# Attention on one core: unnormalised exponentials turned, heads as rows of tokens

## The reference

```python
q = einsum('bnd,hdk->bhnk', layernorm(x), proj_q) + bias_q      # k, v the same from the context
logits = einsum('bhqk,bhnk->bhqn', q, k) / 8
attn = softmax(logits, axis=-1)                                  # over 154 keys
heads = einsum('bhqn,bhnv->bhqv', attn, v)
x = x + heads_as_rows(heads) @ w_out.T
x = x + ffn(layernorm(x))       # 4-bit quantised inputs and weights in three products
```

## Time and profile before

| | us |
|---|---|
| median of 3 runs | 429.55 (426.49 to 430.19) |
| the profiled execution | 429.8 |
| its span | 427.9 |

### The profile page before, as it was taken

The page is one execution under the profiler, slowest core; times in us unless marked ns, Lnnn a source line. Parts: engine busy times, 40 slices in busy tenths (PEclk is TensorE's granted clock), DMA queues, the critical chain, the costliest instruction groups (busy, mean ns, idle before and its releaser), DMA issues.

```text
span 427.9 us, 9077 instructions
## 1 busy us (share of the span) xinstructions
PE 337.4 (79%) x3371; PEld 250.3 (58%) x3371; DVE 363.5 (85%) x652; ACT 259.6 (61%) x821; POOL 273.2 (64%) x275
## 2 busy tenths in 40 slices
PE   1865877876969969869687698198877999999985
PEld 1542355665747757757465466076655766677764
DVE  2989558899999997999999969448999999999692
ACT  4756578877787877877884678334351545543331
POOL 3453455897888878978886568613592767686710
PEclk9999589998998979999999669689998999999999
DMA  7970343455554464655543434600000000000001
GB/s 218 323 282 1 63 92 63 82 105 96 93 102 86 93 117 86 109 84 91 106 85 73 93 63 92 123 2 2 2 0 15 12 26 12 21 19 12 27 25 38
DMA packets 92413, 32.44 MB, mean 76 GB/s; under 512 B 84492, under 2 KB 90320, under 8 KB 92369
## 3 DMA queue, kind: packets, MB, share of 16 engines
q1 hardware_dynamic: 92369, 31.86, 34.7%
HBM read 8.78 MB, written 2.10 MB: 25 GB/s over the span
## 4 chain that ended last, share of the span: by engine, by line
DVE 58%; PE 18%; POOL 14%; issue 5%; ACT 3%; DMA 1%; SPq 0%; DVEq 0%; POOLq 0%
DVE negmax L1036 6%; POOL arena L1304 5%; POOL arena L1298 5%; DVE arena L1049 5%; DVE arena L1055 4%; DVE arena L1112 4%; DVE arena L1114 4%; DVE arena L998 3%; PE ps L456 3%; PE ps L458 3%; PE ps L591 3%; PE ps L457 3%; DVE arena L1027 3%; DVE arena L1238 3%; DVE blk_h L1069 2%
## 5 line engine op out<-in xcount | busy, mean ns | idle before, releaser
L805 ACT ACTIVATE arena<-ps,negmax 128x154 f32<-128x154 f32 x256 | 96.5, 395 | 46.8 <-DVE negmax L1036 46.5
L1297 POOL TENSOR_TENSOR arena<-arena,rinv 128x104 f32<-128x104 f32 x64 | 30.1, 470 | 64.5 <-DVE rinv L1042 64.5
L1298 POOL TENSOR_TENSOR arena<-arena,rinv 128x512 f32<-128x512 f32 x64 | 70.5, 1102 | 0.0
L1036 DVE TENSOR_REDUCE negmax<-ps 128x4 f32<-128x616 f32 x64 | 50.2, 785 | 20.5 <-PE ps L591 20.3
L1304 POOL TENSOR_TENSOR arena<-arena 128x640 f16<-128x640 f32 x40 | 63.7, 1592 | 0.8 <-ACT arena L816 0.8
L591 PE MATMUL ps<-kT_h,arena 64*128 64x154 f16 x512 | 39.8, 241 | 28.6 <-DVE arena L1027 18.7
L805 ACT ACTIVATION_READ_ACCUMULATOR arena<-ps,negmax 128x1 f32 x256 | 53.8, 210 | 0.0
L591 PEld LDWEIGHTS ps<-kT_h,arena 64*128 64x128 f16 x512 | 24.0, 98 | 44.9 <-DVE arena L1027 27.0
L456 PE MATMUL ps<-arena,xnT_h 128*128 128x352 f16 x128 | 40.1, 313 | 3.2 <-DVE xnT_l L1122 3.2
L456 PE MATMUL ps<-xnT_h,wq_h 128*128 128x256 f16 x128 | 36.2, 283 | 7.9 <-DVE wot_l L984 2.5
L456 PE MATMUL ps<-arena 128*128 128x256 f16 (+2 forms) x120 | 36.1, 301 | 7.8 <-DVE arena L937 5.9
(11 more groups left out here) (155 smaller groups left out, 1030.5 us busy)
## 6 DMA issues: line engine op xcount, KB each, us to landing
out_dram<-arena SPq DMA_DIRECT2D x16, 128.0 KB, 1.7
xs<-in_x_dram SPq DMA_DIRECT2D x2, 512.0 KB, 7.2
arena<-in_L_xattn_w_out_dram SPq DMA_DIRECT2D x1, 1024.0 KB, 11.8
pT<-arena SPq DMA_TRANSPOSE x64, 3.4
xs<-in_x_dram SPq DMA_DIRECT2D x2, 384.0 KB, 6.6
wffn<-in_L_ffn_w_down_dram SPq DMA_DIRECT2D x1, 704.0 KB, 9.5
wffn<-in_L_ffn_w_gate_dram SPq DMA_DIRECT2D x1, 640.0 KB, 7.8
wffn<-in_L_ffn_w_up_dram SPq DMA_DIRECT2D x1, 640.0 KB, 8.4
```

The source lines that it names most:

```text
L805: last = act.activation(prob[:, j, k * L:(k + 1) * L], ps[:, 2 * (j % 2) + k % 2, (k // 2) * L:(k // 2 + 1) * L], ACT.Exp, bias=negmax[:, ...
L1036: dve.tensor_reduce(negmax[:, s, 4 * j:4 * j + 4].rearrange("p (k u) -> p u k", k=2), v, AX.X, ALU.max, negate=True).then_inc(max_done, 1)
L1298: pool.tensor_tensor(main_of(normal, j), v[:, :, 0:P], r.to_broadcast([P, 4, P]), ALU.mult).then_inc(normed, 1)
```

## The change

Probabilities stay unnormalised: `exps` writes exp(score - max) for each head into 160 columns (154 and 6 zeros), without sums. ACT casts each slot's 128x640 (`high_p`, now all on ACT, from `prob`), POOL subtracts (`low_p`, all on POOL), SP turns it as before, 5 chunks of 128 columns in which heads lie across borders. `norm` and the reciprocals of the sums are gone.

Heads are now made per slot, 5 slots later (`HEADS_LAG`), with the turned probabilities as the weights and the values moving: each chunk meets the one or two heads whose keys it holds (`PARTS`, 8 parts), 66 columns each (64 values, a one, a zero). The result is tokens by heads, with the sum of the exponentials in column 64. DVE takes the reciprocal from there and scales into `hidden_f`; ACT casts, POOL subtracts, and SP turns this with a second DMA transpose (4 tiles of 128x128) into `hidT`. `project(n)` follows 10 slots behind (`PROJ_LAG`), 6 matmuls of 256 columns as before, at the end of PE's slot.

The values are laid out by part, 4 tasks a batch (slots 0 to 3 and 11 to 14). Queries of steps 2 to 7 are one pair a task, one task a slot, into two buffers. The x task comes earlier (slot 8(i-1)-1). The tasks of heads have no high part on ACT.

```diff
+LP = 160
+CHUNK = 4 * LP
+CHUNKS = CHUNK // P
+RING_P = 2 * QUADS
+HB = DK + 2
+HEADS_LAG = 5
+PROJ_LAG = 10
+PARTS = [(c, a) for c in range(CHUNKS) for a in range(4) if c * P < (a + 1) * LP and (c + 1) * P > a * LP]
...
+        def values_at(b, n):
+            return n if b == 0 else 11 + n
+        def wot_at(n):
+            return (6, 8, 9, 10)[n]
         def rows_at(i):
+            return 3 if i == 1 else 8 * (i - 1) - 1
+        def query_at(i, p):
+            return 4 + p // 2 if i == 1 else 8 * (i - 1) + 1 + p
+        def pairs_of(i):
+            return 2 if i <= 1 else 1
...
         def tasks_of(n):
             out = [("x", i) for i in range(1, STEPS) if rows_at(i) == n]
+            out += [t for t in VALUES if values_at(t[1], t[2]) == n]
+            out += [t for t in WOUT if wot_at(t[1]) == n]
+            out += [t for i in range(1, STEPS) for t in query_tasks(i) if query_at(i, t[2]) == n]
+            out += [("h", n - HEADS_LAG)] if HEADS_LAG <= n else []
             out += [("w", k) for k in range(W1_JOBS) if wt_at(k) == n]
...
+        TAIL = {0: [("h", 59), ("h", 60), ("w", W1_JOBS)], 1: [("h", 61), ("h", 62), ("w", W1_JOBS + 1)],
+                2: [("h", 63), ("w", W1_JOBS + 2)]}
+        PROJ_TAIL = {0: (56, 57), 1: (58, 59), 2: (60, 61), 3: (62, 63)}
...
+            def turn_hid(n):
+                i, s, j = place(n)
+                sp.wait_ge(hid_low, n + 1)
+                if n >= RING_P: sp.wait_ge(proj_mm, n - RING_P + 1)
+                sp.dma_start_transpose(hidT[:, j, :, :, s * P:(s + 1) * P].rearrange("p a k n -> p (a k) n"),
+                                       hsplit[:, j]).then_inc(hid_turned[j], 16)
             for n in range(SLOTS):
-                turn_p(n)
+                if n >= 1: turn_p(n - 1)
+                if n >= HEADS_LAG + 2: turn_hid(n - HEADS_LAG - 2)
...
+            def heads(n):
+                i, s, j = place(n)
+                b = batch(i)
+                pe.wait_ge(turned[j], 16 * (n // QUADS + 1))
...
+                o = next_task(("h", n))
+                order = range(CHUNKS)
+                parts = ((v_h, 0), (v_l, 0), (v_h, 1))
+                for k, (v, part) in enumerate(parts):
+                    for c in order:
+                        at = [m for m, (chunk, a) in enumerate(PARTS) if chunk == c]
+                        h0, h1 = PARTS[at[0]][1], PARTS[at[-1]][1] + 1
+                        last = pe.matmul(o[:, h0 * HB:h1 * HB], pT[:, s, j, part, c],
+                                         v[:, b, j, at[0]:at[-1] + 1].rearrange("p m k -> p (m k)"),
+                                         start=k == 0 and c == order[0], stop=k == 2 and c == order[-1], skip_group_check=True)
+                last.then_inc(task_mm, 1)
...
             for n in range(SLOTS):
                 score(n)
-                if parts_of(n): project(*parts_of(n))
                 for t in tasks_of(n):
                     task(t)
+                if n >= PROJ_LAG: project(n - PROJ_LAG)
...
             def slot(n):
                 i, m = divmod(n, 8)
-                if n >= 2 and high_by_act(n - 2): high_p(n - 2)
+                if n >= 1: high_p(n - 1)
+                if n >= HEADS_LAG + 2: high_hid(n - HEADS_LAG - 2)
                 exps(n)
...
             def inverse(n):
+                dve.wait_ge(task_mm, TASK_AT[("h", n)] + 1)
+                dve.reciprocal(rinv[:, n % 2].unsqueeze(2), per_head(n)[:, :, DK:DK + 1]).then_inc(rinv_ready, 1)
+            def scale_hid(n):
+                dve.wait_ge(rinv_ready, n + 1)
+                wait(dve, hid_low, n - 1)
+                dve.tensor_tensor(hidden_f[:, n % 2].rearrange("p (r k) -> p r k", r=4), per_head(n)[:, :, 0:DK],
+                                  rinv[:, n % 2].unsqueeze(2).to_broadcast([P, 4, DK]), ALU.mult).then_inc(task_low, 1)
...
                 row_max(n)
-                if n >= 1: inverse(n - 1)
-                if n >= 2 and not high_by_act(n - 2): high_p(n - 2)
+                if n >= HEADS_LAG + 1: inverse(n - HEADS_LAG - 1)
                 if n >= 1:
                     for t in tasks_of(n - 1):
                         low(t)
-                if n >= 2 and low_by_dve(n - 2): low_p(n - 2)
                 if i == 0: first(n)
-                if m == 3 and i >= 2: add_attention(i - 2)
+                if m == (PROJ_LAG + 8) % 8 and n >= PROJ_LAG + 8: add_attention((n - PROJ_LAG - 8) // 8)
...
             def slot(n):
                 i, m = divmod(n, 8)
                 w = i - 1 if 0 < i <= W_STEPS else None
-                if n >= 1: norm(n - 1)
-                if n >= 2 and not low_by_dve(n - 2): low_p(n - 2)
+                if n >= 1: low_p(n - 1)
+                if n >= HEADS_LAG + 2: low_hid(n - HEADS_LAG - 2)
```

More of the change, by code:

```diff
@@ new lines, in fourth @@
+                def fourth(part, a):
+                    return part.rearrange("p (j r k) -> p r j k", r=4, k=DK)[:, a]
+                for u, (chunk, a) in enumerate(parts_of_values(n)):
+                    out_u = o[:, u * 256:(u + 1) * 256].rearrange("p (j k) -> p j k", k=DK)
+                    keys = slice(chunk * P % LP, chunk * P % LP + P)
+                    for c in range(KC):
+                        three(out_u, cT_h[:, c, b, keys], cT_l[:, c, b, keys], fourth(wv_h[:, c], a), fourth(wv_l[:, c], a),
+                              c == 0, False)
+                    pe.matmul(out_u, ones[:, :], fourth(bv_h, a), start=False, stop=False)
+                    last = pe.matmul(out_u, ones[:, :], fourth(bv_l, a), start=False, stop=True)
@@ L528, in rest_values @@
                 last.then_inc(task_mm, 1)
-            def heads(i, j):
+            def heads(n):
+                i, s, j = place(n)
                 b = batch(i)
-                pe.wait_ge(turned[j], 16 * (2 * i + 2))
-                o = next_task(("h", i, j))
-                parts = ((v_h, vl_h, 0), (v_l, vl_l, 0), (v_h, vl_h, 1))
-                for k in range(2):
-                    for n, (vh, vr, part) in enumerate(parts):
-                        for u in range(2):
-                            h = 4 * j + 2 * k + u
-                            pe.matmul(o[u * DK:(u + 1) * DK, k * 256:(k + 1) * 256], vh[:, b, h * DK:(h + 1) * DK],
-                                      pT[:, i % 2, j, part, 2 * k + u], start=n == 0, stop=False)
-                        for u in range(2):
-                            last = pe.matmul(o[u * DK:(u + 1) * DK, k * 256:(k + 1) * 256], vr[:, b, j, 2 * k + u],
-                                             pT[:, i % 2, j, part, 4], start=False, stop=n == 2)
-                last.then_inc(task_mm, 1)
@@ L547, in project @@
-            def project(i, p):
-                pe.wait_ge(task_low, TASK_AT[("h", i, p // 2)] + 1)
-                if p == 0: wait(pe, proj_done, i)
-                for s in range(2):
-                    o = ps[:, PROJ_BANK, s * D:(s + 1) * D]
-                    a_h, a_l = hidT_h[:, p, s * P:(s + 1) * P], hidT_l[:, p, s * P:(s + 1) * P]
+                pe.wait_ge(turned[j], 16 * (n // QUADS + 1))
+                if i % (STEPS // B) == 0 and s == 0 and j == 0:
+                    pe.wait_ge(task_low, TASK_AT[("v", b, 3)] + 1)
@@ new lines, in heads, with project @@
+                last.then_inc(task_mm, 1)
+            def project(n):
+                i, s, j = place(n)
+                pe.wait_ge(hid_turned[j], 16 * (n // QUADS + 1))
+                if n < QUADS: pe.wait_ge(task_low, TASK_AT[("wo", n)] + 1)
+                if s == 0 and j == 0: wait(pe, proj_done, i)
+                o = ps[:, PROJ_BANK, s * D:(s + 1) * D]
+                for k in range(2):
+                    p = 2 * j + k
+                    a_h, a_l = (hidT[:, j, part, k, s * P:(s + 1) * P] for part in range(2))
@@ L583, in score @@
                 if s == 0:
-                    pe.wait_ge(task_low, TASK_AT[("q", i, j)] + 1)
+                    pe.wait_ge(task_low, TASK_AT[("q", i, 2 * j + 2 - pairs_of(i))] + 1)
                 wait(pe, exp_done, m - 1)
+                q_h, q_l = (queries(i)[:, part] for part in range(2))
                 for k in range(2):
@@ L621, in task @@
                         pe.wait_ge(ones_ready, 1)
-                    values(t[1], t[2]) if t[2] < 2 else rest_values(t[1])
+                        pe.wait_ge(ctx_wide, 1)
+                    values(t[1], t[2])
             turn_x(0)
             pe.wait_ge(w_low, 2)
-            for j in range(QUADS):
-                query(0, j)
+            for t in query_tasks(0):
+                query(0, t[2])
             pe.wait_ge(job_low, J_END)
@@ L700, in _ @@
             turn_xq(0, 1)
-            for p in range(4, PAIRS):
-                project(STEPS - 2, p)
+            for n in range(PROJ_BODY, PROJ_TAIL[0][0]):
+                project(n)
             steps(pe, ffn, first=3)
@@ L849, in slot @@
                     high(t)
[L850 to L852 removed]
+                if n == 2: act.wait_ge(ln_step, 2 * LN_STEPS)
```

(8 more changed lines are left out.)

347 lines of the change are left out of this document (163 added, 184 removed).

## The result

The changed kernel takes 450.22 us (median of 4, 447.9 to 455.7) against 429.72 us (426.49 to 430.19) for the kernel before beside it: 1.048 of its time, 95% interval 1.040 to 1.056. Slower, and about 9 us more than the 441 forecast, inside the range. Executions of one and the same program differ with the clock that TensorE was granted: here 447.9 us at a mean of 0.966, 452.3 (the profiled one) at 0.951 and 455.7 at 0.944, and a ratio leaves out those more than 1.5% above the fastest.

A forecast was written before the change was run, and what follows sets the result against it. DVE's pace bounds the regular attention now; afterwards a PE-DVE wait in each slot would. Terms 0 + 15.4 + 7.8 - 4 - 7.7 + 1 = +12.5 on 429.8 give 442, stated as 441 us; range 418 to 463.

The forecast's parts named there:

- The loop: Slots 16 to 47: heads wait for VectorE's query subtraction, which waits for the score; slot 3.49 us, +8 over four steps.
- H: TensorE time of a slot's 15 short heads matmuls: taken as 0.8 us, bounds 0.67 and 1.63.
- special slots: In each step, the slot with the x task takes 4.15 us and the slot after it 4.35.
- block scales: VectorE's three instructions a step for the weights may not quite fit its new gap: 0.3 us a step.
- the dear matmuls: Rival: short heads matmuls cost more, H = 1.15, +21 us, 462; chance 0.17 together with transposes as the bound.
- Slots 5 to 15: Attention's early slots, with values tasks in 11 to 14 inside the new loop: 55.8 us against 40.42, +15.
- Up to slot 0: Start: 0 us in the sum; POOL's new memsets and copies at worst some 3 us, kept for the range.
- Slots 48 to 62: Attention's last slots, one step with the second layer norm, then seven more: 55.5 us against 59.52, -4.
- The turn and the tail: Turn to the feed-forward: shorter wait, -4.9, and projection of fewer slots, -2.8; tail +1 for POOL.
- The sum: Whole kernel: the terms give +12.5 us on the profiled 429.8.
- What was hidden: Per step, ACT at most 28 us and POOL below 29; SP's transposes 1.9 to 2.7 us a slot; none ends a wait.
- the loop doesn't decide: Rival: slots fall to the next bound, POOL, ACT and DMA, 3.2 us with some loss; 420 us, chance 0.25.

The follow-up runs named there:

- e1: Changed kernel with TensorE doing the projection before the slot's tasks, except in a step's first slot: 423.24 us, ratio 0.986 to the kernel before.
- e2: Changed kernel with VectorE subtracting the parts of tasks issued before heads ahead of the row maxima: 414.82 us, ratio 0.968 to the kernel before.
- e4: Changed kernel with ten short heads matmuls a slot instead of fifteen, one of three products left out: 451.26 us, ratio 1.042 to the kernel before.
- e6: Changed kernel with six more 256-column matmuls on TensorE behind the score of each of slots 5 to 13: 448.06 us.
- e3: Changed kernel without the DMA transposes of the normalised heads, so the projection's input isn't computed: 446.79 us, ratio 1.039 to the kernel before.
- e5: Changed kernel with the second batch's four values tasks in slots 1 to 4 instead of 11 to 14: 444.94 us, ratio 1.026 to the kernel before.
- e9: e8 without the DMA transposes of the normalised heads, so the projection's input isn't computed: 410.48 us.
- e7: Control: kernel before with all subtractions of the previous slot's tasks, heads included, ahead of the row maxima: 451.87 us, ratio 1.050 to the unedited one.
- e8: Changed kernel with the edits of e1, e2 and e5 together: 412.25 us, ratio 0.958 to the kernel before.
- e10: e8 with the projection back behind heads and, in one-query-one-heads slots, ScalarE's query activation ahead of the exponentials: 414.11 us, ratio 0.960 to the kernel before.

## Why the prediction was right in kind, and 9 us short

**The loop.** "So nothing of heads(n-5), project(n-10) and score(n+1) can start before score(n) has gone through DVE" was right, and e1 and e2 show it. The regular slot is 3.50 for 3.49, the step 29.73 for 29.7, slots 16 to 47 +7.8 for +7.8. It is partly luck in the parts: **H** is 0.73, not 0.8, while the subtraction's end reaches TensorE after 0.15 us, not 0.06. The step's special slots came out at 4.15 and 4.36 (4.15 and 4.35). The block scales, for which I added 0.3, fit into VectorE's gap; instead the first projection of a step waits for the attention's sum, +0.2, a wait that I had not named.

**H and the dear matmuls.** The rival fell. The groups of heads' matmuls:

```profile
L564 PE MATMUL ps<-v_h,pT 128*128 128x66 f16 x256 | 49.7, 195 | 27.1 <-DVE q_odd L1062 13.6 <-DVE arena L1062 8.9 <-DVE arena L1086 4.6
...
L564 PE MATMUL ps<-v_h,pT 128*128 128x132 f16 x384 | 44.7, 226 | 0.0
```

Their 195 and 226 ns are durations that overlap; what counts is the spacing, 0.73 us for 15, 49 ns each, and e4 gives the same: 0.24 us for five. The score, with its loads of 128 columns, was the right neighbour row.
The Trainium skill, "TensorE: Matmul & The Clock Gate", section Back-to-back issue gap, has about 81 ns for such a pair at 128 columns. The measurement decides: 49 ns at 66 and 132 columns.

**Slots 5 to 15: +21.5 for +15.4, the step that failed.** The step of the prediction that failed is the clock: every matmul of these slots was priced at full clock. The chain of each slot was right. Windows of slots 7, 8, 11 and 12 of the changed kernel:

```profile
63.82:70.58 6.76, 5.03 (x43) 3.83 (x43) 2.58 (x7) 3.96 (x11) 2.09 (x3) 0.75 0.82 116
70.58:75.36 4.78, 3.04 (x32) 2.44 (x33) 2.58 (x6) 2.92 (x8) 3.23 (x3) 0.76 0.49 96
...
83.83:91.83 8.00, 6.42 (x55) 4.16 (x55) 2.19 (x6) 3.29 (x9) 2.30 (x3) 0.79 0.45 59
91.83:98.34 6.51, 4.88 (x55) 3.42 (x55) 2.25 (x7) 3.84 (x10) 1.03 (x2) 1.00 0.38 73
```

Slot 12, all at 2.4 GHz, takes 6.51 us, as worked out (6.3 to 6.8); slot 11, with part of it at 1.2 GHz (mean 0.79), takes 8.00. In e6 slots 7 and 11 have the full clock, and six matmuls more:

```profile
63.06:68.20 5.14, 4.18 (x50) 3.38 (x49) 2.58 (x6) 3.58 (x10) 2.03 (x2) 1.00 0.69 128
...
80.51:86.96 6.45, 5.64 (x62) 3.93 (x61) 2.19 (x6) 3.29 (x9) 2.02 (x3) 1.00 0.38 75
```

5.14 us where I had 5.0, and 6.45. It is not the filler that makes slot 7 short: e1, e3 and e5 have none, a clock of 1.00 there, and 5.14 or 5.15 us. Each of the eleven slots ran at 1.00 in one of the two profiles; taking it from there gives 2.65 + 4.55 + 5.14 + 3.84 + 3.70 + 4.76 + 6.45 + 6.51 + 7.04 + 6.61 + 5.09 = 56.3, against my 55.8. The other 5.6 us are four slots of the changed kernel (7, 8, 11 and 13) at 0.75 to 0.80. I had said that of the clock "a little may come back". In slots 16 to 47 and 48 to 62 it did (0.94 to 1.00, 0.86 to 0.97); here the opposite came, 0.96 to 0.89. The stretch takes 59.1 us at a mean of 0.96 (e6), 61.9 at 0.89, 66.2 at 0.84 (e3, its longest execution), 67.7 at 0.74 (e4, likewise, with fewer matmuls), and with less waiting in it 53.5 at 0.99 (e1) and 45.4 at 0.98 (e2). What makes the clock fall in one slot of the same program and not in another is open. Standing alone doesn't tell: TensorE stood 1.57 us in slot 11, and some 1.3 us later its matmuls came at half pace; it stood 1.63 us in slot 12 and 1.66 us in the regular part, and the clock stayed:

```profile
149.90 0.27 PE L485 MATMUL ps<-xnT_odd,wq_h 128*128 128x256 f16 x1 [1.66 <-DVE xnT_even L1124]
```

**Up to slot 0: +2.4 for 0.** Also the clock, not the new memsets. The changed kernel's matmuls of the keys, and its first query matmul:

```profile
18.30 0.36 PE L487 MATMUL ps<-arena 128*128 128x308 f16 x1
18.49 0.29 PE L485 MATMUL ps<-arena 128*128 128x308 f16 x1
...
24.51 0.28 PE L485 MATMUL ps<-xnT_even,wq_h 128*128 128x256 f16 x1 [2.25 <-POOL wq_l L1332]
```

and in e1, whose program is the same up to there:

```profile
14.90 0.39 PE L486 MATMUL ps<-arena 128*128 128x308 f16 x1
15.12 0.30 PE L487 MATMUL ps<-arena 128*128 128x308 f16 x1
...
23.12 0.27 PE L485 MATMUL ps<-xnT_even,wq_h 128*128 128x256 f16 x1 [1.60 <-DVE xnT_even L1126]
```

Two things come together. The keys' matmuls start every 0.26 us until 18.3 us in the changed kernel, until 15.2 in the kernel before and 14.9 in e1, and every 0.13 us from there. Then TensorE stands 2.25 us instead of 1.6, and a second spell at half pace follows, 15 matmuls from 25.31 to 28.29 us; the kernel before and e1 have none. The column of the granted clock shows only the second spell: it says 1.00 before 18.3 us too, though the spacing is twice that of full clock.

All twelve profiles fall into these two groups. Where the rise came at 14.6 to 15.6 us, there is no second spell, the column's mean is 1.00 and the first row maximum starts at 31.2 to 31.8 us (kernel before, e1, e5, e6, e9). Where it came at 16.6 to 18.3, the spell follows, the mean is 0.95 and the first row maximum starts at 33.0 to 34.1 (changed kernel, e2, e3, e4, e7, e8, e10). e7 has the kernel before's program there: the 2.4 us are a matter of the execution, and GpSimd's new work was hidden as I said.

**Slots 48 to 62: -4.7 for -4.** Right in the sum, by luck in the parts: slots 48 to 55 take 29.4 us where I had 31.7, so the second layer norm, priced at +2, cost next to nothing (slots 52 to 55 take 3.57 or 3.58 us each), and slots 56 to 62 take 25.4 where I had 23.8.

**The turn and the tail: -4.5 for -6.7.** 10.5 to 6.05 us (I said 5.6), then 6.86 to 4.97, -1.9 where I took -2.8: the twelve matmuls left came at 0.21 us each, at half clock, while of the 24 before the last six had come at 0.11. The tail lost 1.9 instead of 1.0: from the first gate product on VectorE to the fifth it is 34.4 us instead of 32.7, and behind it the two kernels are alike.

**The sum.** The profiled spans differ by 10.1 us more than the +12.5 worked out: 6.1 from slots 5 to 15, 2.4 from the start, 2.2 from the turn and the tail, 0.2 from slots 0 to 4, less 0.7 from slots 48 to 62. The executions at 447.9 us, with a mean clock of 0.966, were not profiled; they lie 7 us above the forecast, and how those 7 divide isn't known.

**What was hidden.** VectorE works 18.1 us of a step (I said some 20), ScalarE 22.4 (at most 28), GpSimd 20.4 (at most 29). All had room, and e3 showed it of the transposes, which I had at 1.9 to 2.7 us a slot and which take 2.7.

**The rival "the loop doesn't decide"** (420) lost, but its number is what the kernel takes once the loop is gone: 423 and 415 in e1 and e2. As it came the change is 4.8% slower; with its own work in another order (e8) it is 4.2% faster than the kernel before.

## What to carry to other kernels

When a change cuts tasks into smaller ones, count again how far back in the list a buffer's last user now lies: with the same three banks, "three tasks earlier" went from two or three slots back to one, and that made two engines wait for each other in each slot. Such a loop is removed at either end, by work that fills the wait or by emptying the bank before the instruction that depends on the other engine; try both, their gains don't add up. And price matmuls behind a wait at half clock as well as at full: in slots 5 to 15 that was some 6 us, in slots 16 to 47 nothing.
